# Per-graph scales and offsets formed on GpSimd, node masks read from PSUM, last four steps of 480 columns, and a batch gather in two steps

## The reference

```python
A = (adj != 0)
h = x                                    # (16, 512, 128)
for l in range(5):
    m = einsum('bnd,de->bne', h, weight[l])
    agg = einsum('bij,bid->bjd', A, m)
    r, z = sigmoid(i_r + h_r), sigmoid(i_z + h_z)
    n = tanh(i_n + r * h_n)
    h = (1 - z) * n + z * h
x1 = layernorm(x + h * nodemask[..., None])
x2 = layernorm(x1 + graph_net(x1, adj))  # five groups of nodes among the first 25, two convolutions each
```

## Time and profile before

| | |
|---|---|
| median of 3 runs | 503.38 us (502.33 to 504.62) |
| the profiled execution | 503.91 us, of which 502.2 us lie between its first and last instruction |
| PE busy | 486.9 us, 97% of the span, 2313 matmuls |
| DVE busy | 375.8 us, 75% |
| ACT busy | 297.1 us, 59% |
| POOL busy | 318.6 us, 63% |
| mean granted TensorE clock | 0.995 of full speed |

### The profile page before, as it was taken

One profiled execution on the slowest core, in us unless ns is written; L12 is line 12 of the kernel. 1 busy time (PEld: TensorE's weight loads), 2 busy tenths in 40 slices (PEclk: granted clock), 3 DMA queues, 4 the chain that ended last, 5 costly groups with the idle time before them and its releaser, 6 DMA issues.

```text
span 502.2 us, 7158 instructions
## 1 busy us (share of the span) xinstructions
PE 486.9 (97%) x2313; PEld 230.8 (46%) x2313; DVE 375.8 (75%) x711; ACT 297.1 (59%) x522; POOL 318.6 (63%) x314
## 2 busy tenths in 40 slices
PE   7999999999999999999999999999989999999994
PEld 4344444444444444444444444434434444564564
DVE  3867867697857688998789878878664878545795
ACT  4546655645565666666567665566653656745564
POOL 3654775758775687776696567869652546324465
PEclk9999999999999999999999999999998999999999
DMA  8768253665525357345937565352242331322313
GB/s 276 229 166 170 44 151 66 175 114 152 146 44 168 84 120 175 83 84 124 209 72 180 146 145 146 64 104 45 42 103 43 63 69 42 63 61 43 78 44 85
DMA packets 131620, 55.44 MB, mean 110 GB/s; under 512 B 95145, under 2 KB 123262, under 8 KB 131582
## 3 DMA queue, kind: packets, MB, share of 16 engines
q1 hardware_dynamic: 106204, 31.86, 30.9%
q10 hardware_dynamic: 25378, 23.12, 15.2%
HBM read 27.70 MB, written 4.19 MB: 64 GB/s over the span
## 4 chain that ended last, share of the span: by engine, by line
PE 78%; DVE 11%; ACT 3%; issue 2%; DMA 2%; POOL 2%; SPq 1%; POOLq 0%; ACTq 0%; DVEq 0%
PE pA L757 23%; PE pR L764 6%; PE pR L762 6%; PE pR L763 6%; PE pZ L764 6%; PE pZ L763 6%; PE pZ L762 6%; PE pHN L762 3%; PE pHN L763 3%; PE pHN L764 3%; PE pIN L762 3%; PE pIN L764 3%; PE pIN L763 3%; DVE T L1354 2%; DVE T L1358 2%
## 5 line engine op out<-in xcount | busy, mean ns | idle before, releaser
L757 PE MATMUL pA<-A,NAT 128*128 128x512 fp8e4 x640 | 152.7, 381 | 0.6 <-DMA NAT<-HT 0.3
L520 POOL TENSOR_TENSOR HT<-H,HT 128x512 f16<-128x512 f32 x74 | 89.1, 1205 | 100.3 <-ACT HT L1126 100.0
L509 POOL TENSOR_TENSOR ZH<-Z,H 128x512 f32<-128x512 f32 x80 | 102.8, 1286 | 38.4 <-ACT Z L1139 36.9
L1354 DVE SCALAR_TENSOR_TENSOR T<-pHN,BHN,R 128x512 f32<-128x512 f32 x80 | 59.9, 749 | 70.8 <-ACT R L1132 70.5
L1143 ACT ACTIVATE pIN<-T,COLS 128x512 f32<-128x512 f32 x80 | 55.4, 692 | 76.3 <-DVE T L1358 76.2
L757 PEld LDWEIGHTS pA<-A,NAT 128*128 128x128 f16 x640 | 62.4, 98 | 76.5 <-issue 1.9
L1126 ACT ACTIVATE HT<-H 128x512 f16<-128x512 f32 x74 | 46.7, 631 | 63.3 <-DVE H L1367 63.2
L1363 DVE SCALAR_TENSOR_TENSOR pIN<-Z,pIN 128x512 f32<-128x512 f32 x80 | 55.1, 689 | 22.5 <-ACT pIN L1143 22.4
L1132 ACT ACTIVATE R<-pR,BRZ 128x512 f32<-128x512 f32 x80 | 54.5, 681 | 27.7 <-PE pR L764 27.1
L1349 DVE TENSOR_TENSOR AG<-pA,AG 128x512 f16<-128x512 f32 x80 | 54.7, 684 | 9.6 <-ACT AG L1122 9.6
L1367 DVE TENSOR_TENSOR H<-ZH,pIN 128x512 f32<-128x512 f32 x80 | 54.9, 687 | 4.2 <-POOL ZH L509 1.6
(11 more groups left out here) (282 smaller groups left out, 832.3 us busy)
## 6 DMA issues: line engine op xcount, KB each, us to landing
AS<-in_adj_dram ACTq DMA_DIRECT2D x13, 1024.0 KB, 6.1
XR<-in_x_dram ACTq DMA_DIRECT2D x16, 256.0 KB, 2.9
XS<-in_x_dram ACTq DMA_DIRECT2D x13, 256.0 KB, 3.2
out_dram<-Y SPq DMA_DIRECT2D x16, 192.0 KB, 2.2
AS<-in_adj_dram SPq DMA_DIRECT2D x2, 1024.0 KB, 8.7
AS<-in_adj_dram SPq DMA_DIRECT2D x4, 256.0 KB, 6.0
NAT<-HT SPq DMA_TRANSPOSE x64, 3.1
XS<-in_x_dram SPq DMA_DIRECT2D x3, 256.0 KB, 7.7
```

Of the source, the lines that this page charges most:

```text
L509: g_.tensor_tensor(ZH[:, :], Z[:, :], H[:, b, :], ALU.mult).then_inc(zh_p, 1)
L520: g_.tensor_tensor(HT[:, b, 1, :], H[:, b, :], HT[:, b, 0, :], ALU.subtract).then_inc(h_lo, 1)
L757: last = mm(pA2[:, k % 2, :], NAT[:, k % 2, h, i, :], A8[:, b, i, :], start=(h == 0 and i == 0), stop=(h == 1 and i == NI - 1))
L1354: v.scalar_tensor_tensor(out=T[:, :], in0=pHN[:, :], scalar=BHN[:, 0:1], in1=R[:, :], op0=ALU.add, op1=ALU.mult).then_inc(t_v, 1)
```

## The change

Six edits.

- Graphs 0 to 11: GpSimd's `inverse_root(b)` now starts at the means and variances (f_mv). It forms the two variances with eps, the inverse roots, the products of mean and scale, and their negatives NB, in six instructions with three waits on its own results between them. VectorE no longer forms VE, NB or X1 for these graphs.
- ScalarE's `normalise(b)` of these graphs stands at FINAL + SCALED instead of one step later, and begins with the X1 rows (a fifth activation, 32x128); it waits for NB from GpSimd. The batch stages A01 and A2 wait for these rows (f_x1).
- The node masks are copied once to the last 64 columns of bank pF (step 9), and `masked` of graphs 0 to 9 reads them from there; `back(10)`, which overwrites pF, waits for the last of them.
- Steps 76 to 79 run their gates, state and candidate on columns 32 to 511 (COLS_OF): 18 of the 26 matmuls of a step, and the elementwise operations. `aggregate` and the copies of the messages keep 512 columns.
- GpSimd gathers BDA's groups two at a time in steps 59 and 60 instead of one at a time in 59 to 62; the stages prep, A01 and A2 move up a step, to (62, 0), (64, 0) and (70, 1).
- `state_lo(75)` goes ahead of `early_messages(77)` on GpSimd; `variances(b)` waits for f_nb of graph b - 4.

```diff
-BATCH_AT = {"prep": (63, 0), "A01": (65, 0), "A2": (71, 1), "B0": (72, 0), ...
+BATCH_AT = {"prep": (62, 0), "A01": (64, 0), "A2": (70, 1), "B0": (72, 0), ...
+COLS_OF = [slice(S if t >= K - Q else 0, N) for t in range(K)]
+        MASKP = pF[:, N - B * NI:N].rearrange("p (b i) -> p b i", b=B)
...
             def inverse_root(b):
...
-                pool.wait_ge(f_var, b + 1)
+                if b < E0:
+                    pool.wait_ge(f_mv, b + 1)
+                    g_.tensor_scalar(VE[:, w, 0:NI], MV[:, w, :, 1], 1.0 + EPS, EPS * EPS, ALU.mult, ALU.add)
+                    g_.tensor_scalar(VE[:, w, NI:NI + 1], MV[:, w, 0:1, 1], EPS, None, ALU.add).then_inc(f_sc, 1)
+                    pool.wait_ge(f_sc, 3 * b + 1)
+                    g_.tensor_tensor(RS[:, w, :], VE[:, w, :], NHALF[:, 0:NI + 1], ALU.pow).then_inc(f_sc, 1)
+                    pool.wait_ge(f_sc, 3 * b + 2)
+                    g_.tensor_tensor(VE[:, w, 0:NI], MV[:, w, :, 0], RS[:, w, 0:NI], ALU.mult)
+                    g_.tensor_tensor(VE[:, w, NI:NI + 1], MV[:, w, 0:1, 0], RS[:, w, NI:NI + 1], ALU.mult).then_inc(f_sc, 1)
+                    pool.wait_ge(f_sc, 3 * b + 3)
+                    g_.tensor_scalar(NB[:, w, :], VE[:, w, :], -1.0, None, ALU.mult).then_inc(f_nb, 1)
+                    return
+                pool.wait_ge(f_var, b - E0 + 1)
                 g_.tensor_tensor(RS[:, w, :], VE[:, w, :], NHALF[:, 0:NI + 1], ALU.pow).then_inc(f_rs, 1)
...
-                elif 59 <= k < 59 + G - 1:
-                    g, j = k - 58, 0
+                elif 59 <= k < 61:
+                    for g in ((1, 2), (3, 4))[k - 59]:
+                        j = 0
...
                 if k == BATCH_AT["sum"][0] + 1:
                     inverse_roots_batch()
+                if SPLIT[k - 1] and k >= EARLY - 2:
+                    state_lo(k - 1)
...
                 pe.wait_ge(h_v, FINAL[b] + 1)
                 if b == BY_DMA:
                     pe.wait_ge(g_dv, 1)
+                    pe.wait_ge(f_ym, BY_DMA)
...
                 elif stage == "A2":
-                    pe.wait_ge(f_nb, TAIL * Q)
+                    pe.wait_ge(f_x1, TAIL * Q)
...
             def normalise(b, blocks=range(NI)):
                 w = b % 4
                 act.wait_ge(f_nb, b + 1)
+                if b < E0:
+                    n = b % Q
+                    fn(X1[S * n:S * n + S, b // Q, :], Y[0:S, w, 0, :], ACT.Identity,
+                       bias=NB[0:S, w, NI:NI + 1], scale=RS[0:S, w, NI:NI + 1]).then_inc(f_x1, 1)
+                    blocks = list(blocks)[1:] + [0]
                 for i in blocks:
+                    if b < E0 and i == 0:
+                        act.wait_ge(f_x1, b + 1)
                     last = fn(Y[:, w, i, :], Y[:, w, i, :], ACT.Identity,
                               bias=NB[:, w, i:i + 1], scale=RS[:, w, i:i + 1])
...
-                    if k == FINAL[b] + SCALED[b] + 1:
+                    if k == FINAL[b] + SCALED[b] and b < E0:
                         normalise(b)
...
             def masked(b):
                 if b < BY_DMA:
                     dve.wait_ge(f_sum, b + 1)
-                    src = YM[:, :, :]
+                    src, mask = YM[:, :, :], MASKP
...
             def variances(b):
                 w = b % 4
                 dve.wait_ge(f_st, b + 1)
+                if b >= 4:
+                    dve.wait_ge(f_nb, b - 3)
...
                 last.then_inc(f_mv, 1)
+                if b < E0:
+                    return
...
-                v.tensor_scalar(X1[S * n:S * n + S, b // Q, :], Y[0:S, w, 0, :],
-                                MV[0:S, w, 0, 0:1], RS[0:S, w, NI:NI + 1],
-                                ALU.subtract, ALU.mult).then_inc(f_nb, 1)
...
-                    if k == FINAL[b] + SCALED[b] and b < E0:
-                        scales(b)
```

More of the change, by code:

```diff
@@ L84 @@
 WIDE = P + PACK
-BATCH_AT = {"prep": (63, 0), "A01": (65, 0), "A2": (71, 1), "B0": (72, 0), "B1": (72, 1), "S": (73, 0),
+BATCH_AT = {"prep": (62, 0), "A01": (64, 0), "A2": (70, 1), "B0": (72, 0), "B1": (72, 1), "S": (73, 0),
             "T": (73, 1), "D": (74, 0), "sum": (75, 0)}
@@ L344, in graph_net_kernel @@
         f_nb = sem("f_nb")
+        f_sc = sem("f_sc")
+        f_x1 = sem("f_x1")
         f_on = sem("f_on")
@@ L566, in prepare_batch @@
                     g_.tensor_copy(BDA[:, :, 0:P].rearrange("p c (q n) -> p c q n", q=Q), BD[:, 0, 0:TAIL, :, :])
-                elif 59 <= k < 59 + G - 1:
-                    g, j = k - 58, 0
[L569 to L572, removed]
+                elif 59 <= k < 61:
+                    for g in ((1, 2), (3, 4))[k - 59]:
+                        j = 0
+                        dst = BDA[:, :, P + SLOT[g - 1]:P + SLOT[g]].rearrange("p c (q j) -> p c q j", q=Q)
+                        for run in runs_of(GROUPS[g]):
+                            last = g_.tensor_copy(dst[:, :, :, j:j + len(run)], BD[:, g, 0:TAIL, :, run[0]:run[-1] + 1])
+                            j += len(run)
                     if g == G - 1:
@@ L700, in _ @@
                         halves(b)
-                if SPLIT[k - 1]:
+                if SPLIT[k - 1] and k < EARLY - 2:
                     state_lo(k - 1)
@@ L761, in split_product @@
             def split_product(bank, w_hi, w_lo, v_hi, v_lo, start, stop):
-                mm(bank[:, :], w_hi, v_hi, start=start, stop=False)
-                mm(bank[:, :], w_hi, v_lo, start=False, stop=False)
-                return mm(bank[:, :], w_lo, v_hi, start=False, stop=stop)
+                mm(bank, w_hi, v_hi, start=start, stop=False)
+                mm(bank, w_hi, v_lo, start=False, stop=False)
+                return mm(bank, w_lo, v_hi, start=False, stop=stop)
             def gates_of_state(k, between=lambda: None):
                 b = GRAPH[k]
-                ht = [HT[:, b, h, :] for h in range(2)]
+                cs = COLS_OF[k]
+                ht = [HT[:, b, h, cs] for h in range(2)]
                 if k < 2:
@@ L775, in gates_of_state @@
                     pe.wait_ge(t_v, k)
-                split_product(pHN, WH[:, 0, 2, :], WH[:, 1, 2, :], ht[0], ht[1], True, True)
+                split_product(pHN[:, cs], WH[:, 0, 2, :], WH[:, 1, 2, :], ht[0], ht[1], True, True)
                 if k > 0:
                     pe.wait_ge(sig_r, k)
-                split_product(pR, WH[:, 0, 0, :], WH[:, 1, 0, :], ht[0], ht[1], True, False)
+                split_product(pR[:, cs], WH[:, 0, 0, :], WH[:, 1, 0, :], ht[0], ht[1], True, False)
                 between()
@@ L799, in first_gates_of_state @@
                 first_messages()
-                split_product(pZ, WH[:, 0, 1, :], WH[:, 1, 1, :], hi, lo, True, False)
+                split_product(pZ[:, :], WH[:, 0, 1, :], WH[:, 1, 1, :], hi, lo, True, False)
             def gates_of_messages(k, between=lambda: None):
-                l = LAYER[k]
-                ag = [AG[:, k % 2, h, :] for h in range(2)]
+                l, cs = LAYER[k], COLS_OF[k]
+                ag = [AG[:, k % 2, h, cs] for h in range(2)]
                 wc = [[WC[:, l, h, g, :] for g in range(3)] for h in range(2)]
@@ L1352, in candidate @@
             def candidate(k):
+                cs = COLS_OF[k]
                 dve.wait_ge(sig_r, k + 1)
-                v.scalar_tensor_tensor(out=T[:, :], in0=pHN[:, :], scalar=BHN[:, 0:1], in1=R[:, :],
+                v.scalar_tensor_tensor(out=T[:, cs], in0=pHN[:, cs], scalar=BHN[:, 0:1], in1=R[:, cs],
                                        op0=ALU.add, op1=ALU.mult).then_inc(t_v, 1)
@@ L1357, in candidate @@
                 dve.wait_ge(in_mm, k + 1)
-                v.tensor_tensor(T[:, :], pIN[:, :], T[:, :], ALU.add).then_inc(u_v, 1)
+                v.tensor_tensor(T[:, cs], pIN[:, cs], T[:, cs], ALU.add).then_inc(u_v, 1)
             def new_state(k):
+                cs = COLS_OF[k]
                 dve.wait_ge(n_a, k + 1)
-                v.scalar_tensor_tensor(out=pIN[:, :], in0=Z[:, :], scalar=1.0, in1=pIN[:, :],
+                v.scalar_tensor_tensor(out=pIN[:, cs], in0=Z[:, cs], scalar=1.0, in1=pIN[:, cs],
                                        op0=ALU.subtract, op1=ALU.mult).then_inc(e_v, 1)
@@ L1408, in masked @@
                     dve.wait_ge(f_sum, b + 1)
-                    src = YM[:, :, :]
+                    src, mask = YM[:, :, :], MASKP
                 else:
+                    mask = MASK
                     dve.wait_ge(f_mm, b - BY_DMA + 1)
@@ L1413, in masked @@
                     src = BACK_BANKS[b][:, :].rearrange("p (i d) -> p i d", i=NI)
-                v.tensor_tensor(YM[:, :, :], src, MASK[:, b, :].unsqueeze(2).to_broadcast([P, NI, D]), ALU.mult).then_inc(f_ym, 1)
+                v.tensor_tensor(YM[:, :, :], src, mask[:, b, :].unsqueeze(2).to_broadcast([P, NI, D]), ALU.mult).then_inc(f_ym, 1)
             def stats_of_rows(b):
@@ L1438, in scales @@
             def scales(b):
[L1439 to L1445, removed]
```

(9 more changed lines are left out.)

26 lines of the change are left out of this document (15 added, 11 removed).

## The result

The changed kernel takes 519.62 us (median of 6 runs, 518.12 to 522.46) against 503.75 for the one before beside it (6 runs, 501.49 to 505.07). The ratio is 1.033, with an interval of 1.029 to 1.037. The profiled execution of the changed kernel took 519.68 us, 517.9 of them between its first and last instruction; before it was 502.2.

A forecast was written before the change was run, and what follows sets the result against it. TensorE, back to back at 5.61 us a step, was taken to bound the kernel. 503.9 less 3.7, 2.0, 1.7 and 1.1 gave 495.4; plus 17.9 of new waits and 3.4 of clock, 516.7, given as 516 us, range 507 to 524.

The forecast's parts named there:

- Off VectorE: TensorE's pauses where VectorE works off layer norms: gone with VE, NB and X1 moved away, 3.7 us saved.
- The gather: At stage prep: TensorE's wait for GpSimd's gather goes, 2.0 us, and the lower clock behind it, 1.7 us.
- 480 columns: Last four steps: 18 shorter matmuls a step save 0.97 us, with the last elementwise chain 1.1 in all.
- The chain behind ZH: GpSimd's small operations and power from ZH's end to NB: 2.37 us, so NB at p + 7.91.
- Bare graphs: Graphs 4, 7, 8, 9 and 10, without additions: TensorE's pHN 0.7 us late each, 3.5 in all.
- Graphs 9 and 10 "cancel": Four extra TensorE transposes, about 0.4 us, ahead of pHN and graph 10's later statistics were let cancel; 0.7 us each kept.
- Graph 11: A2 in TensorE's queue in step 70 waits for graph 11's X1: 2.9 us.
- The clock: Lower TensorE clock after two of the four longest new waits, 1.7 us each: 3.4 us.
- rival (b): Whole kernel: same forecast without the clock's part, 512.8 us; chance 0.2.
- Rival (a): ScalarE's wait is hidden, NB by p + 7.2 (p: start of TensorE's pHN): faster, 494.9 us; chance 0.1.
- Rival (c): VectorE's relief does nothing, TensorE's pauses came from GpSimd and stay: 519.9 us; chance 0.08.
- Rival (d): HT 2.5 us late delays the transposing DMA; TensorE waits for messages at three or four places: about 519; chance 0.12.

The follow-up runs named there:

- two kernels with the same idle time: Kernel before with only VectorE's relief (normalise at its old place), and kernel before with only the masks read from PSUM: 498.87 us and 502.78 us.
- the kernel with the relief alone: Kernel before with only variances, scales and NB on GpSimd and X1 on ScalarE, normalise at its old place: 498.87 us, ratio 0.991.
- the kernel with the longer chain: Changed kernel with two more GpSimd operations, multiplications by 1, between the products and NB of each graph: 532.26 us.

## Why the prediction was right, and where its terms were off

The mechanism was the forecast one at every joint: the wait of ScalarE, R behind it, T behind R, PE behind T, A2 in addition. The time was 519.6 us where 516 was given. That the two lie so near is in part luck: the new waits were 22.0 us instead of 17.9, and the clock's part, taken at 3.4, was 1.6 in the profiled execution. Term by term:

- **Off VectorE, 3.7 us.** Right in the sum with both edits: 4.0 (a third place, step 46, had been left out with its 0.3). The step that gave all of it to VE, NB and X1 was a little too simple: alone they bring 3.1.
- **The gather, 2.0 + 1.7.** Right for the profiled execution, 3.8. But the second part is there in about half of the executions of before only, and two kernels with the same idle time show the full clock behind it.
- **480 columns, 1.1.** 0.6 by the two kernels beside each other (the kernel with the relief alone, with all 512 columns, already ends 0.3 sooner than before, from step 76 on); step 78 didn't get shorter, so something other than its 18 matmuls set it. What, was not tried.
- **NB to T, 4.0 us.** 3.94 in the timeline above (from 196.19 to 200.13), and up to 4.09 in other graphs.
- **The chain behind ZH, 2.37 us.** This was mis-sized: 2.64 (from the end of first_state at 193.55 to 196.19). I let the first operation start 0.05 ahead of ZH's end, and it starts 0.08 behind it, since it waits for the statistics; and I let pairs follow at 0.17, where at the front the second one started 0.27 behind the first and took 0.24. Twelve times 0.27 are 3.2 us, the largest single miss.
- **Bare graphs at 0.7.** Graph 8 took 0.95, graph 4 0.97: 0.7 + 0.27. Graph 7 took 1.79, and graph 3 2.39 instead of 1.25, since a cast fell on GpSimd's operations. For graph 3 this is shown; for graph 7 the trace has the state's low half beside a cast at 1.74 us instead of 1.16, which was not tried by itself. No row of before could show this one: there the cast began 1.16 us behind the low half, and with less work on VectorE it begins only 0.06 behind.
- **Graphs 9 and 10 "cancel".** They did in the sum only: 0.12 and 1.35. Both had the extra transposes ahead of pHN, 0.44 us. For graph 9 ScalarE also had no HT between Y and R, since the step ahead was a last layer, and NB to T took 3.56 us instead of 3.94; for graph 10 GpSimd waited 0.80 us for the late statistics.
- **Graph 11, 2.9.** 3.26 by the steps. Here too GpSimd waited for the statistics, 0.87 us.
- **The clock, two of four waits, 3.4.** One, 1.6, in the profiled execution, where rival (b), no clock loss at all, was about as near as the forecast. Of the six executions three had a mean granted clock of 0.995 and took 518.1 to 519.7 us, one had 0.992 and 519.6, and two had 0.989 and took 520.9 and 522.5, so there are executions with more of it.

The terms that were too small (the chain 3.2, the casts 1.5) outweigh those that were too large (the clock 1.8, first_state at 1.3 instead of 1.12, graph 9). Rival (a) needed NB no later than p + 7.2; it came at p + 9.3 (p = 186.89, graph 0), and even a bare graph is a full microsecond from that point. Rival (c) (its 519.9 should be 516 + 3.7 = 519.7) falls with the six cured steps of the kernel with normalise a step later. Rival (d) falls by the changed kernel's list of waits, where PE waited for a transposed NAT once, 0.4 us.

## What to carry to other kernels

An engine's queue is a place in time: work handed to another engine must be due where its consumer already stands with everything that it needs behind it. Before moving a consumer up, write down when the last producer ends and what is queued behind the consumer; here 1.3 us of slack stood against a delay of some 2 us or more, twelve times. All six edits with the later place of normalise and A2 beat both kernels, 495.5 to 495.8 us.

## What the runs showed of the hardware that was not expected

In the changed kernel small operations on GpSimd (all but the power, which takes 1.20 us for five elements) cost 0.19 to 0.27 us whatever their size from one to five elements, and as much as 0.73 beside a cast on VectorE; a waited one starts some 0.08 us behind its producer.

An idle time of TensorE of 1.9 us was followed by the lower clock in one profiled execution and not in those of two other kernels at the same place of the program, and the mean clock of the kernel before was 0.993 or 0.994 in 16 of 33 executions. With waits of up to 4 us, as in the kernel with the longer chain, the lower clock cost some 5 us beyond the waits by the medians and 7 by the profiles: delays of a few microseconds on TensorE can cost more than themselves, and a single profile doesn't tell how often.
